# Moving the slot map, the eighth window's projection and some constant products around the experts' entry of an attention and mixture-of-experts layer

## Time and profile before

| | |
|---|---|
| median of three executions | 743.64 us (742.49 to 745.95) |
| the profiled execution, its own time | 746.3 us |
| its span in the trace | 744.5 us |
| PE busy | 666.6 us (90%) |
| DVE busy | 565.8 us (76%) |
| ACT busy | 512.1 us (69%) |
| POOL busy | 307.7 us (41%) |
| mean granted clock of TensorE | 0.976 of full |

### The profile page before, as it was taken

One profiled execution on the slowest core, in us unless ns is written; L12 is line 12 of the kernel. 1 busy time (PEld: TensorE's weight loads), 2 busy tenths in 40 slices (PEclk: granted clock), 3 DMA queues, 4 the chain that ended last, 5 costly groups with the idle time before them and its releaser, 6 DMA issues.

```text
span 744.5 us, 17166 instructions
## 1 busy us (share of the span) xinstructions
PE 666.6 (90%) x5648; PEld 517.6 (70%) x5649; DVE 565.8 (76%) x881; ACT 512.1 (69%) x886; POOL 307.7 (41%) x334
## 2 busy tenths in 40 slices
PE   0686786969999999999999999999988998989995
PEld 0564564847878787778777887888766676767674
DVE  4758899657777777777777787778758879797984
ACT  4665486556767676767676767666756787978885
POOL 3000373422544454445444544454411244656654
PEclk9999798869999999999999999999999999999999
DMA  9894688370111111111111111111136777976740
GB/s 289 262 241 163 155 287 279 87 254 28 54 45 49 49 51 47 49 49 49 49 50 49 49 49 49 49 49 48 51 103 188 219 228 197 265 212 188 202 158 29
DMA packets 66351, 92.56 MB, mean 124 GB/s; under 512 B 6432, under 2 KB 53408, under 8 KB 66304
## 3 DMA queue, kind: packets, MB, share of 16 engines
q1 hardware_dynamic: 57872, 70.40, 31.7%
q0 software_dynamic: 6864, 18.75, 7.9%
q10 hardware_dynamic: 1568, 2.76, 1.2%
HBM read 59.06 MB, written 32.83 MB: 123 GB/s over the span
## 4 chain that ended last, share of the span: by engine, by line
PE 64%; DVE 11%; ACT 9%; issue 8%; DMA 3%; POOL 3%; SPq 1%; ACTq 0%; DVEq 0%; POOLq 0%
PE PS L1266 57%; PE PS L1516 4%; DVE SMALL L960 3%; ACT WORK L803 3%; PE PS L1494 2%; DVE XN L1122 1%; ACT QS L798 1%; DVE WALL L954 1%; DMA XN<-in_x 1%; POOL OTS L603 1%; DVE WORK L1032 1%; DVE WORK L1025 1%; DMA KS<-parts_scratch 1%; DVE WALL L978 1%; ACT WORK L731 1%
## 5 line engine op out<-in xcount | busy, mean ns | idle before, releaser
L370 DVE TENSOR_TENSOR WS<-WALL,WS 128x1024 fp32r<-128x1024 f32 x144 | 176.4, 1225 | 91.1 <-ACT WS L886 90.5
L1266 PE MATMUL PS<-WS,XTS 128*128 128x512 f32 x852 | 236.4, 413 | 2.4 <-DVE XTS L954 2.3
L1266 PEld LDWEIGHTS PS<-WS,XTS 128*128 128x128 f32 x852 | 151.6, 191 | 46.8 <-DVE XTS L954 14.9
L886 ACT ACTIVATE WS<-WALL 128x1024 fp32r x144 | 152.2, 1058 | 41.5 <-issue 39.3
L1266 PE MATMUL PS<-WALL,WORK 128*128 x568 | 136.2, 383 | 0.8 <-ACT WORK L902 0.8
L666 POOL DMA_INDIRECT WORK<-xn_scratch,WORK x72 | 101.2, 1406 | 31.6 <-issue 21.4
L1266 PEld LDWEIGHTS PS<-WALL,WORK 128*128 128x128 f32 x568 | 102.2, 190 | 12.9 <-issue 1.0
L603 POOL TENSOR_TENSOR OTS<-SIDE,XN 128x256 f32<-128x256 f32 x31 | 26.2, 845 | 195.7 <-DVE XN L1122 116.1
L670 POOL DMA_INDIRECT ys_scratch<-SIDE,WORK x36 | 42.0, 1165 | 118.6 <-ACT SIDE L912 118.6
L960 DVE TENSOR_REDUCE SMALL<-PS 128x8 f32<-128x1024 f32 x64 | 77.4, 1209 | 13.5 <-PE PS L1266 12.9
L803 ACT ACTIVATE WORK<-PS 128x512 f32<-128x512 f32 x128 | 69.4, 595 | 20.3 <-PE PS L1266 16.6
(11 more groups left out here) (142 smaller groups left out, 1008.6 us busy)
## 6 DMA issues: line engine op xcount, KB each, us to landing
WALL<-in_wexp SPq DMA_DIRECT2D x28, 384.0 KB, 7.0
WALL<-ys_scratch SPq DMA_DIRECT2D x16, 512.0 KB, 7.0
parts_scratch<-WORK SPq DMA_DIRECT2D x32, 240.0 KB, 2.4
QS<-parts_scratch SPq DMA_DIRECT2D x16, 480.0 KB, 4.5
XN<-in_x SPq DMA_DIRECT2D x4, 1024.0 KB, 12.3
xn_scratch<-XN SPq DMA_DIRECT2D x4, 1024.0 KB, 7.5
WALL<-in_x SPq DMA_DIRECT2D x8, 512.0 KB, 5.6
KS<-parts_scratch SPq DMA_DIRECT2D x16, 240.0 KB, 3.8
```

What stands on the lines that cost most here:

```text
L370: eng.tensor_tensor(out=WS[:, 1 - k, half, 1], in0=weights, in1=WS[:, 1 - k, half, 0].bitcast(F32), op=ALU.subtract).then_inc(low_ready[ha ...
L886: act.activation(WS[:, 1 - k, half, 0], weights, ACT.Copy).then_inc(high_ready[half], 1)
L1266: return pe.matmul(o, a, b, start=start, stop=stop)
```

## The change

1. `MAP_UNIT` goes from 4 to 3, and `slot_map()` is called behind `project()` of its unit, so between unit 3's projection and unit 4's `values`. DVE calls `take_map()` and `finish_map()` together in unit 4, behind that unit's `take_max` and `invert`. PE waits for `map_taken` in unit 5 as before.
2. Window 7 is inverted and divided in halves of 128 columns, as the last window of the kernel already is. Its `project()` leaves the end of batch 1 and stands on PE behind `tokens(0)` and `tokens(1)`. On DVE its addition stands behind `low_xt(1)`.
3. Each `keep` has a semaphore of its own. ACT waits for `rows_out[0]` ahead of `high_part(1,1,0)`, DVE for `rows_out[1]` ahead of `low_part(1,1,0)`. `high_part(0,0,1)` moves behind the two `take_xt`.
4. `keep_warm` is new on PE: products of the identity and WOUT into a free PSUM bank, 256 columns each, of which nothing is read. Two stand at the end of batch 1, three behind the tokens and three behind the projection.

```diff
-MAP_UNIT = 4
+MAP_UNIT = 3
...
+            def divide_halves(w):
+
+                pool.wait_ge(sides_ready, 2 * w + 2)
+                pool.wait_ge(r_full, w)
+                for k in range(NC_D):
+                    pool.wait_ge(recip_ready, w + 1 + (w >= EXTRA * NWIN) + k)
+                    pool.tensor_tensor(out=OTS[:, k, :], in0=SIDE[:, k * P:(k + 1) * P],
+                                       in1=DENS[:, k * P:(k + 1) * P], op=ALU.mult).then_inc(turned_ready, 1)
...
             gather(1)
             divide(6)
-            divide(7)
+            divide_halves(7)
...
                 high_part(0, 0, 0)
-                high_part(0, 0, 1)
...
                 take_xt(0, 0)
                 take_xt(1, 1)
-                act.wait_ge(rows_out, 16 * EXTRA)
+                high_part(0, 0, 1)
+                act.wait_ge(rows_out[0], 16)
                 high_part(1, 1, 0)
...
-                        if u == MAP_UNIT:
+                        if u == MAP_UNIT + 1:
                             take_map()
-                        if u == MAP_UNIT + 1:
                             finish_map()
...
-                    if last and u == UNITS - 1:
-                        invert_last()
+                    if ends(b) and u == UNITS - 1:
+                        invert_halves()
...
-                if ends(b):
-                    if not last:
-                        invert()
+                if last:
                     project(b, NWIN - 1)
...
                 low_part(dve, 0, 0, 0)
-                dve.wait_ge(r_free, c["R"].now() + 1)
...
                 low_xt(0, 0)
                 low_xt(1, 1)
+                project(EXTRA - 1, NWIN - 1)
+                dve.wait_ge(r_free, c["R"].now() + 1)
                 low_part(dve, 0, 0, 1)
+                dve.wait_ge(rows_out[1], 16)
                 low_part(dve, 1, 1, 0)
...
-                    if first == 1 and u == MAP_UNIT:
-                        slot_map()
-                    if first == 1 and u == MAP_UNIT + 1:
+                    if first == 1 and u == MAP_UNIT + 2:
                         pe.wait_ge(map_taken, 1)
                     if u % 2 == 1 and (u > 1 or (b and b != EXTRA)):
                         project()
-                if ends:
+                    if first == 1 and u == MAP_UNIT:
+                        slot_map()
+                if last:
                     project()
+
+            def keep_warm(o, n):
+
+                for _ in range(n):
+                    mm(o, IDF[:], WOUT[:, 0, :])
...
-                pe.wait_ge(r_full, c["R"].now())
+                pe.wait_ge(w_free, c["W"].now() + 1)
+                keep_warm(W_BANK[:, 0:D], 2)
...
                 tokens(0, 0)
                 tokens(1, 1)
+                keep_warm(W_BANK[:, 0:D], 3)
+                project()
+                keep_warm(W_BANK[:, 0:D], 3)
                 up(0, 0, 0)
```

More of the change, by code:

```diff
@@ L329, in layer @@
         xt_full, xt_high, xt_free = sem("xt_full"), sem("xt_high"), sem("xt_free")
-        rows_out = sem("rows_out")
+        rows_out = [sem(f"rows_out{b}") for b in range(EXTRA)]
         high_ready = [sem("high_ready0"), sem("high_ready1")]
@@ L483, in keep @@
                 t = slice(b * TB, (b + 1) * TB)
-                sp.dma_start(rv[:, t, :], XN[:, t, :]).then_inc(rows_out, 16)
+                sp.dma_start(rv[:, t, :], XN[:, t, :]).then_inc(rows_out[b], 16)
             begin(0)
@@ L496, in _ @@
             keep(1)
-            sp.wait_ge(rows_out, 16 * EXTRA)
+            for b in range(EXTRA):
+                sp.wait_ge(rows_out[b], 16)
             sp.wait_ge(y_stored, 1)
@@ L600, in divide @@
                 pool.wait_ge(sides_ready, 2 * w + 2)
-                pool.wait_ge(recip_ready, w + 1)
+                pool.wait_ge(recip_ready, w + 1 + (w >= EXTRA * NWIN))
                 wait_some(pool, r_full, w)
@@ L698, in _ @@
                         divide(b * NWIN + n)
[L699 to L704, removed]
+            divide_halves(B * NWIN - 1)
         @block.scalar
@@ L808, in sides @@
                 act.wait_ge(o_full, n)
-                wait_some(act, turned_ready, n - 1)
+                wait_some(act, turned_ready, n - 1 + (n > EXTRA * NWIN))
                 act.activation(SIDE[:], O_SUMS, ACT.Copy).then_inc(sides_ready, 1)
@@ L1122, in invert, with invert_halves @@
                 dve.reciprocal(out=DENS, in_=DENS).then_inc(recip_ready, 1)
-            def invert_last():
+            def invert_halves():
                 n = c["O"].add()
@@ L1400, in project @@
             def project():
-                pe.wait_ge(turned_ready, c["R"].now() + 1)
-                pe.wait_ge(r_free, c["R"].now() + 1)
+                n = c["R"].now()
+                before = n + (n >= EXTRA * NWIN)
+                pe.wait_ge(turned_ready, before + 1)
+                pe.wait_ge(r_free, n + 1)
                 for ch in range(NC_D):
-                    if c["R"].now() == B * NWIN - 1 and ch:
-                        pe.wait_ge(turned_ready, B * NWIN + ch)
+                    if n in (EXTRA * NWIN - 1, B * NWIN - 1) and ch:
+                        pe.wait_ge(turned_ready, before + 2)
                     last = mm(R_BANK[:, 0:D], OTS[:, ch, :], WOUT[:, ch, :], ch == 0, ch == NC_D - 1)
@@ L1436, in batch @@
             def batch(b, first=None):
-                par, last, ends = b % 2, b == LAST, b in (EXTRA - 1, LAST)
+                par, last = b % 2, b == LAST
                 for u in range(UNITS):
```

## The result

Eight executions of the changed kernel took 746.86 to 752.03 us, median 749.78, against 745.03 for the kernel before in the same comparison: ratio 1.0059, 95% interval 1.0037 to 1.0081, so 4.4 us slower (2.8 to 6.0). A second comparison on another occasion gave 1.0064 (1.0039 to 1.0089). The profiled execution took 752.03 us, the slowest of the eight, and its span is 750.2 us, 5.7 us longer than before. In it the mark, the start of up(1,1,1), is at 176.52 against 170.68, 5.8 us later: the whole difference is made before the experts' loop reaches its pace.

What follows compares the result with a forecast made beforehand. PE bounds the experts' loop, so only when it reaches its pace counts: weights 1.7 us later plus entry 3.8 make 5.5 us, forecast 749.1 us from a median of 743.64; range 743.0 to 753.0.

Steps and rivals of the forecast that it cites:

- the delay of the weights: Map, one unit earlier: DVE's take_max and reciprocal precede the copy, so the last weights are issued 1.7 us later.
- the upper end: Map: the idle 1.6 us may cost PE its clock, making the weights 3.8 us later.
- rival (c): Second loss of clock, before the map or behind up(0,0,1): 2 to 4 us more, 752 to 753; chance 0.14.
- PE stands idle for 1.6 us: Ahead of the map: projection ends at 135.00, POOL's places at 136.54, so the map starts at 136.6.
- The halves and the units 5 to 7: Window 7's halves and batch 1's shifted units before the tokens: hidden, cost and gain 0.
- The cover: End of batch 1: last projection at some 155, several microseconds before the tokens; 3 us left without the weights' delay.
- The entry: From tokens to up(1,1,1): +3.8 us, bounds +1.5 and +5.4, including half a microsecond for the clock's return.
- T: Start of the tokens' transposes, released by the last weights: 159.66 before, 161.4 forecast.
- the landing: Second store at the entry: lands 4.6 us after issue, bounds 4.2 and 5.7, delaying low_part(1,1,0).
- (a): Places ready early, 2.4 GHz back soon after T: slower by only 1.6 to 3.7 us; chance 0.24 with (d).
- (b): Second store at the entry as good as free, landing under 2.7 us at full clock: 743.0; chance 0.16.
- (d): Products keep the clock through the wait for weights; faster entry, store still behind projection; chance 0.24 with (a).

Runs made afterwards that it cites:

- run 8: As run 6, but without the eight constant products, the projection staying behind the tokens; ratio 1.0003 to the kernel before.
- run 11: The changed kernel with window 7's projection back at the end of batch 1 and without the products; ratio 1.0048 to the kernel before.
- Run 3: The changed kernel with take_map and finish_map ahead of take_max on DVE in unit 4; ratio 1.0004 to the kernel before.
- run 6: As Run 3, and POOL writes its second eight places ahead of divide(4); ratio 1.0005 to the kernel before.
- run 5: The changed kernel with window 7's projection back at the end of batch 1, products kept; ratio 1.0023 to the kernel before.
- Run 4: The changed kernel without any of the eight constant products; ratio 1.0056 to the kernel before.
- run 7: As run 6, with window 7's projection back at the end of batch 1 and no products; ratio 0.9985 to the kernel before.
- run 1: The changed kernel with the map's matmuls, take_map and finish_map in their old places; ratio 1.0023 to the kernel before.
- run 2: The kernel before with only the map moved behind unit 3 and take_map and finish_map in unit 4; ratio 1.0045.
- run 9: As run 7, with ACT's last three groups of places one unit earlier; ratio 0.9950 to the kernel before.

## Why the prediction was right

The forecast was 5.5 us more than before, from the right two places; measured were 4.4. The profiled execution was to take 751.8 us and took 752.03. That agreement to 0.2 us is luck, twice over: two sizes were off against each other, and the execution that was profiled is the slowest of its eight. The median, 749.78, is close to the forecast 749.1 because the forecast added 1.1 us too much to a median of three that lay 1.4 us under the later one of eight.

**The map.** The mechanism came as written: the wait for POOL's places, then take_max and the reciprocal in front of the copy. From take_max to the reciprocal's end it is 3.29 us as reckoned. Mis-sized was the delay of the weights, 3.84 us instead of 1.7. It is the upper end that I had given for a loss of clock in the map, also named in rival (c), and that is what happened: the map took 1.63 us longer, with 0.85 and 0.65 granted in it. The step that failed is "PE stands idle for 1.6 us": it was 3.37. I had taken unit 3 at the speed of the kernel before, where the clock was 0.50 and the projection took 2.01 us. In the changed execution it took 1.13, so PE came earlier to a wait whose end didn't move (136.74 against 136.6 reckoned). Of the eight traces with 2.79 to 3.61 us of idle time in front of it, the map took 5.8 us or more in seven; the exception is the one with 2.79 (run 8). In the six with 1.6 us or less it took 4.2, and one of them, run 11, is the changed program up to there. That fits the idle time as what cost the clock; no run set the idle time alone. The copy and its steps took 0.3 us more than the 2.24. The tokens started 3.42 us later, because the weights took 12.7 us from issue to tokens instead of 13.2.

**Window 7.** The halves and the units 5 to 7 were hidden, as costed: PE was done with batch 1 at 159.3 and waited 3.75 us for the weights. The cover was thinner than costed, though. The last projection of batch 1 started at 157.33, where I had 155, and with weights 3.84 us earlier the tokens would have come at 159.2, less than 1 us behind its end and not 3. Run 3, which removed the delay of the weights, did find the attention units in its way.

**The entry.** PE entered at 1.2 GHz as forecast, the tokens took 0.9 us, the three products 2.6, the projection 1.9, ending at T + 5.35 instead of 6.3. From there to the store 0.49 us (0.48 reckoned). The projection's early end is worth 0.5 us beyond the half that I had allowed for the clock. The larger miss is the landing: low_part(1,1,0) started 3.70 us after the issue, under my lower bound of 4.2, where I had taken 4.6. Here two measures were mixed. The times of the earlier trace rows run to the landing of the data, while the 5.7 I had as the upper bound runs to the start of the engine that waits. The same view of the changed kernel has, for its two stores and two loads:

```profile
DMA to landing us min/median/max: 2.9/4.3/9.9
```

The 2.9 is the second store, which had landed in 5.0 us in the kernel before, and DVE started 0.8 us behind that landing. So in the measure of the earlier trace rows the store took 2.9 instead of 4.6, and 0.8 us from the landing to its waiter were missing from the sum. By that measure one of my signs of being wrong, a store landing in under 3 us, did appear. The Trainium skill ("DMA: Bandwidth & Descriptors", section "Anatomy of one DMA — SWDGE (gpsimd) path") gave an estimate of 3.2 us, for another issuing path; both measured values are nearer to it than to the 4.6 that I took from the earlier trace rows. From low_part(1,1,0) to the mark 3.90 us, as reckoned. In all +2.4 instead of +3.8: 0.5 from the projection and 0.9 from the store, up to its waiter.

**The rivals.** (a) and (b) didn't happen; runs 6 and 8 show that even at 2.4 GHz the store is not free, since DVE still waits 1.7 to 1.8 us for it. Of (c) the first place came true: the map lost the clock, which cost 1.6 us, and the shorter entry hid it in the total. (d) was wrong for the changed kernel: two products ahead of a pause of 3.75 us didn't hold the clock. It held where the pause was 0.8 us with products (run 5), but also where it was 1.73 us without any (run 8), so these two don't show that products hold it.

Not settled is why the weights take between 12.1 and 13.7 us from issue to tokens in kernels in which they are what comes last; no run varied that. Run 4 leaves open what the products are worth in the changed kernel itself.

## What to carry to other kernels

An operation moved earlier only pays if what reads its result moves too: look at what stands in front of the reader on the reader's own queue, and at what comes last before the operation, on every engine that feeds it, since moving one supplier shows the next. Before work is moved out of one wait into another stretch, ask which transfer is issued behind it; here the projection cost less than 1 us before the tokens (run 7 against run 8), and behind them it held a store, and through it the second expert tile, which made the entry 1.4 us longer. And before two traces are compared by absolute times, look where they stood when they reached the edit.

## What the runs showed of the hardware

The clock state at a place in the program is not a property of the program up to there. Up to unit 3's projection the changed kernel, its repeat, the kernel before and runs 1 to 5 and 11 are the same, yet that projection took 1.13 us in six of these nine executions and 2.0 to 2.1 in three (the kernel before, runs 1 and 11). An idle stretch of 2.9 to 3.6 us ahead of 64 small matmuls went with 1.6 to 2.1 us more for them in seven traces, so such a wait can cost half again what its row shows; with 2.79 us or less nothing was added in seven. A store of 512 KB on almost idle DMA engines (share 0.22 from 167 to 169 in the changed kernel) let its waiter go 3.7 to 3.8 us after the issue in the seven traces in which it stood behind the tokens, and 4.4 and 4.8 us after it in runs 7 and 9, in which it was issued 0.65 us behind the start of the tokens. In the kernel before, where it was issued 0.5 us before the last weights released the tokens, that was 5.7.
